# Writing the block-diagonal K of an attention stage in two halves, with the engines' orders of work searched anew

## Time and profile before

| | |
|---|---|
| median of three runs | 1279.05 us |
| the profiled execution | 1278.19 us |
| its span, first to last instruction | 1276.3 us |
| PE busy | 1156.3 us (91%) |
| DVE busy | 1044.5 us (82%) |
| ACT busy | 865.6 us (68%) |
| POOL busy | 699.2 us (55%) |
| mean granted TensorE clock | 0.951 |

### The profile page before, as it was taken

How to read it: one execution, slowest core, us unless ns; L and a number is a source line. 1 busy time by engine, 2 the same in 40 slices (tenths; PEclk the granted TensorE clock), 3 DMA queues, 4 the chain that set the end, 5 groups by cost and what they waited for, 6 DMA issues and landing times.

```text
span 1276.3 us, 27899 instructions
## 1 busy us (share of the span) xinstructions
PE 1156.3 (91%) x10338; PEld 833.9 (65%) x10338; DVE 1044.5 (82%) x2837; ACT 865.6 (68%) x1684; POOL 699.2 (55%) x827
## 2 busy tenths in 40 slices
PE   1567578999999999999999999999999998999998
PEld 1344445675767677676767676776757676766775
DVE  3667877989889898989899898989898898768653
ACT  0335455786868686777868676877868685866665
POOL 3202122666464757566574747566664647455775
PEclk9656879999999999999999999999999999999999
DMA  6000001001010101001010101001010101000000
GB/s 198 21 10 12 12 25 29 17 4 43 10 37 17 38 17 37 18 5 43 10 36 18 37 17 37 18 21 33 4 44 9 38 2 37 17 10 17 10 9 9
DMA packets 63847, 32.69 MB, mean 26 GB/s; under 512 B 29281, under 2 KB 63073, under 8 KB 63329
## 3 DMA queue, kind: packets, MB, share of 16 engines
q1 hardware_dynamic: 61696, 26.83, 8.4%
q10 hardware_dynamic: 2016, 4.08, 0.9%
HBM read 24.73 MB, written 4.19 MB: 23 GB/s over the span
## 4 chain that ended last, share of the span: by engine, by line
PE 78%; DVE 10%; POOL 6%; ACT 3%; issue 2%; DMA 1%; SPq 0%; POOLq 0%; DVEq 0%; ACTq 0%
PE py L697 16%; PE pa L543 5%; PE pa L508 4%; PE pg L687 3%; PE pu L687 3%; PE pg L688 3%; PE pg L689 3%; PE pu L688 3%; PE pu L689 3%; PE pa L532 3%; POOL xn L856 2%; PE pa L550 2%; PE pb L590 2%; PE pb L596 2%; PE pa L697 2%
## 5 line engine op out<-in xcount | busy, mean ns | idle before, releaser
L895 POOL TENSOR_TENSOR moe<-moe 128x512 f32<-128x512 f32 x256 | 331.1, 1295 | 293.3 <-DVE moe L1194 179.0
L697 PE MATMUL py<-wd_s,moe 128*128 128x128 f32 x1856 | 250.7, 280 | 0.2
L697 PEld LDWEIGHTS py<-wd_s,moe 128*128 128x128 f32 x1856 | 232.9, 192 | 19.9 <-issue 4.4
L1073 DVE TENSOR_REDUCE q_st<-pa 128x4 f16<-128x480 f32 x256 | 168.4, 658 | 42.1 <-PE pa L508 40.2
L1194 DVE SCALAR_TENSOR_TENSOR moe<-tg,pg 128x512 f32<-128x512 f32 x232 | 157.8, 680 | 49.0 <-ACT tg L818 46.7
L818 ACT ACTIVATE tg<-pg 128x512 f32<-128x512 f32 x232 | 140.2, 604 | 75.2 <-PE pg L689 74.3
L756 ACT ACTIVATE probs<-pa 120x512 f32<-120x512 f32 x256 | 138.9, 598 | 49.4 <-PE pa L532 46.9
L832 ACT ACTIVATE moe<-pu 128x512 f32<-128x512 f32 x232 | 139.2, 600 | 15.9 <-PE pu L689 13.9
L508 PE MATMUL pa<-kbd,qkht 128*128 128x480 f16 x256 | 101.3, 396 | 24.5 <-DVE q_st L1073 19.5
L856 POOL TENSOR_SCALAR xn<-x,lnm,lnr 128x128 f32<-128x128 f32 x192 | 90.0, 481 | 5.2
L687 PE MATMUL pg<-x4h,wg_h 128*128 128x512 f16 x232 | 88.9, 383 | 3.7 <-DVE moe L1194 0.2
(11 more groups left out here) (200 smaller groups left out, 2743.8 us busy)
## 6 DMA issues: line engine op xcount, KB each, us to landing
xin<-in_x SPq DMA_DIRECT2D x16, 256.0 KB, 2.8
xres<-in_x SPq DMA_DIRECT2D x16, 256.0 KB, 3.0
kbd<-qkht SPq DMA_DIRECT2D x256, 7.5 KB
out_x<-acc SPq DMA_DIRECT2D x16, 256.0 KB, 4.2
ctxt_a<-in_ctx_t SPq DMA_DIRECT2D x16, 240.0 KB, 2.7
ctxt_b<-in_ctx_t SPq DMA_DIRECT2D x16, 240.0 KB, 3.4
ctxn_b<-in_ctx SPq DMA_DIRECT2D x16, 240.0 KB, 4.1
wd_s<-in_wd ACTq DMA_DIRECT2D x1, 1024.0 KB, 8.4
```

The source lines that it names most:

```text
L697: mm = pe.matmul(moe_y(g, e)[:, j, :], hu[:, u % 3, j * S:(j + 1) * S], wd_s[:, u, :], start=(half == 0 and j == 0), stop=(half == 1), ski ...
L895: pool.tensor_tensor(hu[:, u % 3, :], gw[:, u % 3, :], us[:, u % 3, :], ALU.mult)\
L1073: dve.tensor_reduce(q_st[:, t, 4 * c:4 * c + 4, 3 * HD], pa[:, BM, 0:4 * SC].rearrange("p (h k) -> p h k", h=4), AX.X, ALU.max, negate=Tru ...
```

## The change

`kbd` is loaded by 32 DMAs for a group in place of 16: 16 for batches 0 and 1 (half 0), then 16 for batches 2 and 3 (half 1), each half the size. Half 0 waits for `qkht` of the group and for the first 8 `max` of the group before, half 1 for all 16. Eight semaphores take the place of four, and on PE `max 2.c` now waits for its quarter of half 1, as `max 0.c` does for its quarter of half 0. All strings of `TURNS` with more than one stage are new on all four engines. The core of the diff:

```diff
-        kbd_in = [signal(f"kbd{c}_in", 16 * HQ) for c in range(4)]
+        kbd_in = [[signal(f"kbd{half}{c}_in", 16 * HQ) for c in range(4)] for half in range(2)]
...
+            def load_kbd(g, half):
+
+                part = slice(2 * half, 2 * half + 2)
+                if later(g):
+                    sp.wait_ge(max_ps.sem, max_ps.at(g - 1, 4 * (2 * half + 2)))
+                for h in range(H):
+                    rows = slice(h * HD, (h + 1) * HD)
+                    keys = qkht2[rows, g % 2, GB * S:GB * (S + SC)].rearrange("p (t k) -> p t k", t=GB)
+                    sp.dma_start(kbd[rows, part, h, :], keys[:, part, :]).then_inc(kbd_in[half][h // HQ].sem, 16)
...
                     sp.wait_ge(qkht_done.sem, qkht_done.at(n))
-                    if n:
-                        sp.wait_ge(max_ps.sem, max_ps.at(n - 1, 4 * GB))
-                    else:
+                    if n == 0:
                         sp.wait_ge(kbd_clear.sem, 1)
-                    for h in range(H):
-                        rows = slice(h * HD, (h + 1) * HD)
-                        sp.dma_start(kbd[rows, :, h, :],
-                                     qkht2[rows, n % 2, GB * S:GB * (S + SC)].rearrange("p (t k) -> p t k", t=GB))\
-                          .then_inc(kbd_in[h // HQ].sem, 16)
+                    for half in range(2):
+                        load_kbd(n, half)
...
                 if name == "max":
-                    if t == 0:
-                        pe.wait_ge(kbd_in[c].sem, kbd_in[c].at(g, 16 * HQ))
-                        if c == 0:
+                    if t % 2 == 0:
+                        pe.wait_ge(kbd_in[t // 2][c].sem, kbd_in[t // 2][c].at(g, 16 * HQ))
+                        if t == 0 and c == 0:
                             pe.wait_ge(qkht_done.sem, qkht_done.at(g))
```

More of the change, by code:

```diff
@@ L67 @@
         "n": "nnnnnnn",
[L68 to L76, removed]
+        "wna": "nnaannaaaaaaaaaaaanaaaaaaaawaaaaanaaaawanwaawaaaaaawaa",
+        "nab": "aaaaaabaaaabbaabaabababbaababnanbaababaabbabnbanaabaaabaabaanbabaanabnbaa",
+        "nabd": "bnabaandbanbaabaaaabdababbdbadnaaaanbaabdbabaadanabababaaabaadabnaabadbabdaaabdabada",
+        "nabdc": ("dcacabccnbacaccaccaacbaaaabaccdaabcbabdccaabcbbaacaadndcccacbbaabcacnbccbaabnccacbacacbcacdbacdb"
+                  "cdcacabacndcaccacbaandncacccbcdbacca"),
+        "abdc": ("cbbacacaccacaacaccbaacacbcdacabbdcaacacacccbdabcbbbcaccdaabcbccacbadcbdabadccabcaaccacaabacdbadc"
+                 "cbaacaccacbccabaccadbcabdacca"),
+        "bdc": "dccbccccdbdcddccccccbdcbccbcccbcccbcbbcccbbdbbcbccbdbccccbcdbcccccbcbcccbcdbccbdccb",
+        "dc": "ccccccccccccccdcccccccdccdccdcdcccccdccdccdccdcccccccdccdcc",
         "c": "cccccccccccccccccccccccccccccccccccccccccccccccc",
@@ L80 @@
         "n": "nnnnnnn",
[L81 to L89, removed]
+        "wna": "nnaaawwnwanaawaaaanawaaaaaaaaaaaaaanaaaaaanaaaaaaaaaaa",
+        "nab": "aaaaaaaababbaaabaaabbabbaaaabaabnbnabaabbbabbaabaaabaanbaaanbanaabnbbnaaa",
+        "nabd": "bnanbadbaanbaabaababadbdabbdaaaaabdaaabdbaaabnanababaababadaaabananabbaadabaabddbada",
+        "nabdc": ("dcaaccbcaccaaabcacbaccabaaccaabdbbacadcabaacnabaccbaacdcncbabbaabbccccaaccbcbccadnacnbdacbacdcbc"
+                  "cadacacdacabnaccacanndcbacccbbcadcca"),
+        "abdc": ("cccaabaaccaccabacbcaccbacacbadaaadcccabaccbbcadcbcabbaccbcadcbbcbdcaacadadbcaccacbcadacbacbaacca"
+                 "acaaccbadbcccacbacaadbcadbcca"),
+        "bdc": "dccccbccdcdbdcccccbcbcccccbbbccbddbcccbbbdccbcbcdbccccbcdcbccbccbccccbccbdccbccbcbd",
+        "dc": "ccccccccccccccccdcccccdccdcccddcdcccdcccccdcccdccccccdccdcc",
         "c": "cccccccccccccccccccccccccccccccccccccccccccccccc",
@@ L93 @@
         "n": "nnnnnnn",
[L94 to L102, removed]
+        "wna": "nnaanaaaananaaaaaanaaaanwaaaaaaawaaaaaaaaaawawaawaaaaa",
+        "nab": "abaaaaabaanaabaababababbaaaabnaabbabbababaabbnabbaaaaaaaababananbabnnabaa",
+        "nabd": "bnadanbabanbaabaaadabbbaanbddaabaabnadaabadbaababadabbnaabnaaabaaaaabadabdbaaabdbada",
+        "nabdc": ("caccbacaacccabadabcbaaacacabbcaacnbcbcacbaacadbaaccddabcncabacbbnccbcacbacadcacaacbacbcdacdnbbcc"
+                  "adcacccdncancnaccbabdcabaaaccccbdaca"),
+        "abdc": ("acccbaccaacabdacccabccadbaacaccbaaacdbcbcabccbcabcbcabbacdacbcaacdbacabbcadcaaccacdcaabcaccdacab"
+                 "daabacacccbaccacabbcdaabdccca"),
+        "bdc": "ddccccdbcccdcbddcbccbccbbcccccbbcccbbbcbccbbcccbccbccccccdbbccbddcbccccccbbcddcccbb",
+        "dc": "cccdcdcccccccccccccdcccccdcccccdcccdcccccdcddcccccccccdcdcc",
         "c": "cccccccccccccccccccccccccccccccccccccccccccccccc",
@@ L106 @@
         "n": "nnnnnnn",
[L107 to L115, removed]
+        "wna": "nnaaanawaananaaaaaaaaaaaanawaawaaawaaawaaaaaanaaaaaaaa",
+        "nab": "abnaaaaanbbaaaabaaaaaaabababnbabbaabaaabbaaanbabaanbabbanbnbaabaaabbabaaa",
+        "nabd": "bbbbaaabndbadbbbbaabbadanabandaaaaaaaaabbdbnaadabadaaaadanbaaaadandbbbaaaabbaadaabna",
+        "nabdc": ("cccbccadcdaabccdacaanaccbdaccabncbcaanaabcbbcacdaabbbabbcbabaaddcaancccccccbbcdccaaacaccaacccbba"
+                  "caaadbaacdccndbbnaancacccacbaccbacaa"),
+        "abdc": ("cacabcacabcdcaaacababaaccbaabbdbbababcaacaacdaabacabacacabddadbccdbaacbccacacabbcbacaacccaacccdc"
+                 "bcaacccdaabcccccccbdccbdccacc"),
+        "bdc": "cdccbccbbcccbbccdcbdbcdcbccbdbbbcbdbcdcbcccccbcbbcbbcccdccccccbccdccdbbcdbccccccccc",
+        "dc": "cccccccccccccdcccdccddcccdcccccccdccccccddccdcdcdcccccccccc",
         "c": "cccccccccccccccccccccccccccccccccccccccccccccccc",
```

## The result

The changed kernel takes 1282.45 us (median of 20 runs, 1278.98 to 1286.12) where the kernel before takes 1279.99 us (20 runs, 1277.56 to 1282.09) on the same chip. The ratio is **1.0017, 95% interval 1.0010 to 1.0025**: slower by 2.2 us, less than the 0.3% that I called no change, but with an interval that does not touch 1. I had said 1277.0; the sum behind it was a gain of 1.1 us. So the change came out small, as I had said, and on the other side of zero. By the experiments, costs of 5.1 and 1.7 us were set off by gains of 2.9 and 1.7 us, so the closeness of the total proves little of my working.

The account below looks back on a forecast made before the run. PE was taken to bound the steady stretch, its turn set by the chain through quant. Steady +1.2, fill -2.0 and drain -0.3 sum to -1.1 us; forecast 1277.0 us, own range 1273 to 1281, 8 in 10 within 1267 to 1287.

Parts of the forecast that it names:

- I take 0.1 us a period: Steady period after its head and K's arrival: 0.1 us slower each, bounds -0.2 and +0.8; +1.2 us over twelve.
- by the rows this is SP's time, which has room: SP's queue: the additional K transfers of 16 groups, 11.6 us each, add nothing to the sum.
- The wait that the split shortens is not the deciding one: SP before K's transfers: the wait for ACT's copy of qkht ended last, so the split's earlier start gains nothing.
- Head of the steady period, gain 0: Steady turn up to max1.1: idle moves from before xit, max1.1 still 12.9 us after g0; gain 0, at most 0.2.
- Arrival of K, 0.35 us to spare: Steady max0.3: K's last quarter lands 14.53 us after qkht, 0.35 before due; value 0, loss up to 0.8 a period.
- Transfers of half the size are no cheaper: K's DMAs on SP: half the size taken as no help, since issue does not go by bytes; 0.73 us each.
- 186 us: Cost of the additional K transfers by the skill's rule alone, 16 groups times 11.6 us; left out of the sum.
- SP's queue late: Rival at xres on POOL, 0.8 us to spare: at 3 us late, 0.8 a period, 1287 us; chance 0.08.
- Fill -2.0: Pipeline fill, nabd period: qkv done before stacks0, gaining 2 to 3 us in batch 0's chain; -2.0, bounds -7 and +4.
- Drain -0.3: Four draining kinds: periods start in the same order up to xit; -0.3 us, bounds -3 and +3.
- POOL's L886 released by a DMA: Sign that would show the forecast wrong: POOL at L886 waiting on a DMA.
- a stop before `max0.3` with a DMA as releaser: Sign that would show the forecast wrong: PE stopped before max0.3, waiting on a DMA.

Follow-up runs that it names:

- orders_only: Changed kernel with K loaded whole by 16 DMAs, all new strings kept; ratio 1.0004 to the kernel before.
- fill_new: Kernel before with the new strings only in wna, nab and nabd, K loaded whole; ratio 0.9987 to the kernel before.
- drain_new: Kernel before with the new strings only in abdc, bdc and dc, K loaded whole; ratio 0.9977 to the kernel before.
- fill_old: Changed kernel with the old strings in wna, nab and nabd, K still in two halves; ratio 1.0064 to the kernel before.
- xn4t_later: Changed kernel with PE's xn4t moved behind u14 in the steady nabdc string; ratio 0.9939 to the kernel before.
- after_xres_xn4t: Changed kernel with xres issued before SP waits for qkht and steady xn4t moved behind u14; ratio 0.9938 to the kernel before.
- orders_xn4t: Changed kernel with K loaded whole and steady xn4t moved behind u14; 1270.90 us against 1280.16, ratio 0.9932 to the kernel before.
- best_a: Kernel before with the new strings in fill and drain, old steady strings, K loaded whole; ratio 0.9966 to the kernel before.
- steady_old: Changed kernel with the old strings in the steady nabdc periods, K still in two halves; ratio 0.9999 to the kernel before.

## Why the prediction was wrong, point by point

**The steps that failed.** The step that turned the sign is "I take 0.1 us a period" for the rest of the steady period: it was about 0.4 us a period, mostly PE's stop of 0.65 us before `xn4t`, a wait that the prediction does not have. The other is "by the rows this is SP's time, which has room", which put the longer queue of SP at nothing: the split costs 10.5 us with the old strings and some 1.7 with the new, through `xres` queued behind K. A drain 2.6 us better than forecast hid part of both.

By the ratios, times 1280 us, the result is this sum. Only fill and drain were measured by themselves (-2.8 to -0.4 and -4.2 to -1.8). The term of the steady strings is `orders_only` (0.5) less `fill_new` and `drain_new`, good to some 2 us; the last is the changed kernel less `orders_only`. So the sum closes by construction. The steady term has a second witness: the usual period is 71.25 us against 70.87, which is 4.6 us in twelve.

| term | forecast | measured |
|---|---|---|
| new strings, fill | -2.0 | -1.7 |
| new strings, steady | +1.2 | +5.1 (a difference) |
| new strings, drain | -0.3 | -2.9 |
| split | 0 | +1.7 (with the old strings +10.5) |
| sum | -1.1 | +2.2 |

- **The wait that the split shortens is not the deciding one**: right, 16 of 16 groups start behind ACT's copy.
- **Head of the steady period, gain 0**: right in each gap, but the gain was 0.2, which I had as its bound. The turn of the earlier trace rows is not a usual one: its period is 71.15 us, its neighbours' 70.87. In the neighbour before it `max1.1` comes 12.65 us after `g0` (513.72 less 501.07), in the changed kernel 12.45 (519.77 less 507.32). My own gaps said as much: 0.31 and 0.76 gone and one of about 0.74 new, with the same steps, leave 0.33 less.
- **Arrival of K, 0.35 us to spare**: right but for the one turn shown. Of the steady periods only that one has a stop for K before `max0.3`, of 0.23 us.
- **Transfers of half the size are no cheaper**: right, 685 ns at the least and 23.3 us for 32, where 16 of twice the size took 11.63. The Trainium skill (DMA: Bandwidth & Descriptors, section Rules for kernel authors) says to join small transfers into one. The trace agrees: the 16 additional ones a group bought no time and took 11.6 us of SP each time. The 186 us that I worked out by that rule from the rows is not what the kernel paid; with the old strings that was 10.5 us, and nothing measurable when the one urgent load went first.
- **"by the rows this is SP's time, which has room"**: this step failed. I checked what is queued behind K on SP only in the steady turn and only with the new strings, where `xres` had 0.8 us to spare. For that turn the working holds: POOL reads it at 597.78 us, 19.2 after `g0`, where I had 19.3, and only three steady periods show a wait, of 0.70 us at most. In the fill the reading of `xres` comes earlier relative to K: POOL stands 8.9 and 10.9 us in `fill_old`, 9.6 in the changed kernel. With the old steady strings it is about 1.1 us late in each period. I had the mechanism as a rival ("SP's queue late", 0.08), but only in the steady turn.
- **"I take 0.1 us a period" for the rest**: this step failed too, and it is the term with the largest error, about 0.4 measured: +0.65 for the stop, -0.2 at the head, the rest small. I counted `xn4t` among the steps that moved ahead of K and asked only when K would be late. I did not ask whether what `xn4t` itself reads was ready: its input leaves POOL 0.65 us after PE gets there.
- **Fill -2.0**: right in size, -1.7. That is in part luck: the stages were argued from one execution, the range was 11 us wide, and the chain of batch 0 that was to give 2 to 3 us was not followed in a trace.
- **1277.0**: the sum gives 1277.1 to 1278.0, and I wrote a number just outside it.
- **Drain -0.3**: wrong by 2.6 us. "The four draining kinds start their periods in the same order up to `xit`" overlooked that in the first of them the stop before `xit` was 2.40 us long, with the fall of the clock behind it. I had looked at the gaps of the fill and of the steady turn, not at this one.
- Of the signs by which I would know: two named against me came, "POOL's L886 released by a DMA" (five times, up to 9.6 us) and "a stop before `max0.3` with a DMA as releaser" (once in the steady periods, 0.23 us). The period is 71.25 us and not 70.9 to 71.0. The other signs came as said: ACT's copy as releaser, a gap of 0.73 us before `max1.1` in place of the one before `xit`, 0.73 us for each transfer.

What stays open: whether the late `xres` still costs anything once the steady strings are right. With it the kernel is at 0.9939 (`xn4t_later`), without it at 0.9938 (`after_xres_xn4t`) or 0.9932 (`orders_xn4t`), with intervals that overlap. The same holds, less so, for the 1.7 us between `orders_only` and the changed kernel: the intervals (0.9995 to 1.0014, 1.0010 to 1.0025) overlap. The traces say more than the times here. The three steady periods of the changed kernel in which POOL waits for `xres` (at 455.05, 669.78 and 883.89 us) last 71.47, 71.90 and 71.57 us where 71.25 is usual. From the fifth group to the last, K's transfers take 785.3 us there and 784.2 in `orders_only`. `xn4t_later` has two such waits, in periods of 72.39 and 70.86 us where 70.50 is usual. So the late load seems to cost 1 to 2 us still, in one execution of each.

## What to carry to other kernels

Splitting a transfer to start a part of it sooner pays only if the split wait was the last to end; what it did here for certain is make the issuing queue longer, so look at each load queued behind it, in each stage and above all in the fill, and put those with no dependence on the split ahead. Where a step is moved up, check two sides: who waits for it, and whether its own input is ready at the new place. Here one step placed 0.65 us too early, in a loop of twelve, hid the whole gain of the new order: moved back, it gave 8 to 10 us.

## What the runs showed that I had not expected

The same strings fill the pipeline in quite different times. With the new strings of the fill, K's transfers of the fifth group, the first of the steady turns, start at 277.18 us in `best_a`, 281.24 in `steady_old` and 285.64 in the changed kernel. Even `best_a` and `fill_new`, which have the same program up to the drain, differ by 5.5 us there (277.18 and 282.68). The clock granted from 60 to 175 us, where PE has much idle time, goes with it: 0.72 in `best_a` and 0.63 in `fill_new`; 0.72 in `xn4t_later` (fifth group at 277.59) and 0.64 in the changed kernel.

```profile
60.00:175.00 115.00, 76.82 (x687) 49.05 (x685) 82.47 (x207) 52.53 (x83) 25.41 (x42) 0.72 0.08 21
```

```profile
60.00:175.00 115.00, 78.56 (x656) 52.60 (x649) 78.75 (x202) 50.84 (x79) 24.04 (x41) 0.64 0.06 14
```

The mean clock of each execution sorts their times as well. Of the 20 of the changed kernel, the seven at 0.958 or more take 1278.98 to 1280.52 us and the thirteen below take 1281.41 to 1286.12. Of the seven of `best_a`, the four at 0.958 or more take 1272.39 to 1274.56, the three at 0.950 take 1277.59 to 1278.31. Whether the clock makes the fill longer or a longer fill lowers the clock is not shown. Either way a difference of 2 us in the fill has to be taken from many runs and not from two traces.

The normalisation on POOL (L861, four pieces) took 1.74 us in the fill and at two places of the steady period (584.22 and 592.38), 3.48 us at the turn, and 2.29 at the turn of the kernel before. DVE being busy does not explain it: it was busy throughout both the 2.29 us and the 1.74 us at 592.38. But the length goes with what DVE does meanwhile. Beside the 3.48 us it runs three operations that read both inputs from SBUF:

```profile
565.29 0.70 DVE L1064 TENSOR_TENSOR qb<-qb,rr 128x512 f32<-128x512 f32 x1
...
566.37 0.69 DVE L1067 TENSOR_TENSOR k_st<-kb,k_hi 120x512 f16<-120x512 f32 x1
566.97 0.69 DVE L1070 TENSOR_TENSOR q_st<-qb,q_hi 128x512 f16<-128x512 f32 x1
```

Beside the 2.29 us there is one of these, beside the 1.74 us at 584.22 and 592.38 none. No run was made to test it, so the cause is not shown; but an order that keeps ln4's normalisation clear of these three might remove the stop of 0.65 us too.
